# The new stage's norms ahead of the late maxima, POOL's scaled copies spread between the triangles, squares laid out by token

## Time and profile before

| | us |
|---|---|
| median of 3 runs | 1517.89 (1513.53 to 1517.95) |
| profiled execution, its time | 1519.11 |
| its span | 1517.4 |
| PE busy | 1147.0 (76%) |
| DVE busy | 997.9 (66%) |
| ACT busy | 618.4 (41%) |
| POOL busy | 444.8 (29%) |
| mean granted TensorE clock | 0.837 of full speed |

### The profile page before, as it was taken

How to read it: one execution, slowest core, us unless ns; L and a number is a source line. 1 busy time by engine, 2 the same in 40 slices (tenths; PEclk the granted TensorE clock), 3 DMA queues, 4 the chain that set the end, 5 groups by cost and what they waited for, 6 DMA issues and landing times.

```text
span 1517.4 us, 18332 instructions
## 1 busy us (share of the span) xinstructions
PE 1147.0 (76%) x5332; PEld 584.4 (39%) x5332; DVE 997.9 (66%) x2391; ACT 618.4 (41%) x1170; POOL 444.8 (29%) x460
## 2 busy tenths in 40 slices
PE   2778888886886976968878540144988988989897
PEld 1334454452543533525444420122443443434343
DVE  3617336475767668657764756888888888988321
ACT  1070733625626436247165310222463454544552
POOL 2030211203304115124041233234535434434220
PEclk7575888897988988979889775567999989989898
DMA  3111010220320401403103137012021021000000
GB/s 104 58 44 63 30 69 9 96 60 2 128 59 31 125 29 44 139 1 127 51 1 81 30 100 210 21 44 51 7 51 38 21 59 34 24 28 1 21 3 12
DMA packets 85333, 79.81 MB, mean 53 GB/s; under 512 B 42768, under 2 KB 62864, under 8 KB 83216
## 3 DMA queue, kind: packets, MB, share of 16 engines
q1 hardware_dynamic: 85264, 79.01, 18.2%
HBM read 43.45 MB, written 35.00 MB: 52 GB/s over the span
## 4 chain that ended last, share of the span: by engine, by line
PE 58%; DVE 20%; issue 9%; ACT 7%; POOL 3%; SPq 1%; DMA 1%; ACTq 0%; DVEq 0%; POOLq 0%
PE ps L1202 13%; PE ps L1188 9%; PE ps L881 5%; PE ps L943 5%; PE ps L913 4%; DVE arena L1693 4%; ACT arena L1342 3%; PE ps L916 3%; PE ps L972 3%; PE ps L932 3%; PE ps L1194 2%; ACT arena L1304 2%; PE ps L1010 2%; PE ps L992 2%; PE ps L1020 2%
## 5 line engine op out<-in xcount | busy, mean ns | idle before, releaser
L1304 ACT ACTIVATE arena<-ps 128x512 f32<-128x512 f32 (+2 forms) x200 | 110.9, 573 | 336.8 <-PE ps L881 214.3
L1693 DVE TENSOR_REDUCE arena<-ps 128x2 f32<-128x1024 f32 (+3 forms) x176 | 194.6, 1125 | 56.7 <-PE ps L916 54.1
L1202 PE MATMUL ps<-arena,late 128*128 128x512 f32 x512 | 225.6, 592 | 0.0
L1342 ACT ACTIVATE arena<-ps 128x1024 f32<-128x1024 f32 (+3 forms) x256 | 170.2, 718 | 38.9 <-PE ps L932 37.4
L712 POOL TENSOR_SCALAR_AFFINE_SELECT arena<-arena 128x512 f32<-128x512 f32 x128 | 84.8, 667 | 286.0 <-ACT arena L1342 285.7
L881 PE MATMUL ps<-ident,arena 128*128 128x128 f32 (+1 forms) x640 | 114.9, 327 | 48.9 <-ACT arena L1304 15.6
L1188 PE MATMUL ps<-arena,late 128*128 128x512 f32 x256 | 133.6, 682 | 12.4 <-ACT arena L1474 12.4
L1202 PEld LDWEIGHTS ps<-arena,late 128*128 128x128 f32 x512 | 96.2, 190 | 115.8 <-issue 115.5
L913 PE MATMUL ps<-kr,qr 32*128 32x512 f32 (+3 forms) x512 | 107.7, 471 | 35.9 <-issue 20.2
L932 PE MATMUL ps<-qr,kr 32*128 32x256 f32 (+3 forms) x512 | 75.8, 447 | 70.1 <-ACT arena L1342 64.8
L943 PE MATMUL ps<-arena 128*32 128x512 f32 (+3 forms) x1024 | 104.2, 494 | 22.6 <-ACT arena L1304 19.4
(11 more groups left out here) (164 smaller groups left out, 1953.6 us busy)
## 6 DMA issues: line engine op xcount, KB each, us to landing
scan_d<-late SPq DMA_DIRECT2D x64, 138.0 KB, 3.1
qr<-q_rep SPq DMA_DIRECT2D x8, 1024.0 KB, 5.7
kr<-k_rep SPq DMA_DIRECT2D x8, 1024.0 KB, 8.1
arena<-scan_d SPq DMA_DIRECT2D x12, 552.0 KB, 6.0
q_rep<-hilo SPq DMA_DIRECT2D x24, 256.0 KB, 3.0
k_rep<-hilo SPq DMA_DIRECT2D x24, 256.0 KB, 3.9
proj_d<-arena SPq DMA_DIRECT2D x8, 768.0 KB, 5.1
late<-proj_d SPq DMA_DIRECT2D x8, 768.0 KB, 4.4
```

Source lines behind the costliest of these rows:

```text
L1202: last = pe.matmul(ps[:, ring2.bank(f"{n}{c}"), :], w[:, k, c * P:(c + 1) * P], src[:, k, :], start=(k == 0), stop=(k == HC - 1))
L1304: return act.activation(dst, src(ps[:, bank, :]), func, **kw)
L1342: act.activation(prob[:, gg % 2, 2 * pr:2 * pr + 2, p_off[jt]:p_off[jt] + w], ps[:, bank:bank + 2, 0:w], ACT.Exp).then_inc(p_taken, 1)
L1693: v.tensor_reduce(heads[:, 2 * pr:2 * pr + 2, gs[0]:gs[-1] + 1], ps[:, 2 * (k % 2):2 * (k % 2) + 2, 0:len(gs) * w].rearrange("p q (n w) -> ...
```

## The change

On DVE, in slots with both `pre` and `b`, `norms_heads(pre)` moves between the third and the fourth token maximum. In slot 8 (no `b`) the four dispatch copies move ahead of `finish(tail)`, and `norms_heads(pre)` behind it. On POOL, `squares(front)` stands ahead of `scale_keys(pre)`, both at (0, 1); the copies stand one to a place from (0, 1) to (1, 1), and the last score products one place earlier. `p_sq` becomes [2 x 64 tokens][8 features]: POOL reads with a stride and writes in order, and DVE's sum reads in order.

```diff
--- before.py
+++ after.py
@@ -240,7 +240,7 @@
         p_fold_m = p_pairs.rearrange("p c n d -> p (c n d)")
         p_gram = co.take(NC, 6)
         p_fold = co.take(NC, 2 * HD)
-        p_sq = Carve(p_over, late).take(2 * HD, TS)
+        p_sq = Carve(p_over, late).take(2 * TS, HD)
 
 
         c1 = Carve()
@@ -716,7 +716,8 @@
 
                 g.wait_ge(pre_loaded, CREDIT + (b + 1) * 32)
                 g.wait_ge(wy_done, CREDIT + b * DVE_WY)
-                g.tensor_tensor(p_sq, p_mix[:, 0:2 * HD, :], p_mix[:, 0:2 * HD, :], ALU.mult).then_inc(l_squared, 1)
+                qk_p = p_mix[:, 0:2 * HD, :].rearrange("p (w d) t -> p w t d", w=2)
+                g.tensor_tensor(p_sq.rearrange("p (w t) d -> p w t d", w=2), qk_p, qk_p, ALU.mult).then_inc(l_squared, 1)
 
             by_time = lambda j: p_mix[:, j * HD:(j + 1) * HD, :].rearrange("p d t -> p t d")
             along = lambda r: r.unsqueeze(2).broadcast_to([P, TS, HD])
@@ -727,6 +728,8 @@
                 g.wait_ge(norms_done, CREDIT + (b + 1) * DVE_NORMS)
                 g.wait_ge(pre_stored, CREDIT + b * (N2 * 16))
                 g.tensor_tensor(p_kc, by_time(1), along(p_rk), ALU.mult).then_inc(l_kb, 1)
+
+            def fold_keys(b):
                 g.tensor_tensor(p_wu[:, :, 0:HD], by_time(1), along(p_rb), ALU.mult).then_inc(l_kb, 1)
 
             def scale_values(b):
@@ -759,23 +762,27 @@
                     for jt in range(NT):
                         if i is not None:
                             causal(i, gg, jt)
+                        if front is not None:
+                            if (gg, jt) == (0, 1):
+                                squares(front)
                         if pre is not None:
-                            if (gg, jt) == (0, 0):
+                            if (gg, jt) == (0, 1):
                                 scale_keys(pre)
+                            if (gg, jt) == (0, 2):
+                                fold_keys(pre)
                             if (gg, jt) == (0, 3):
                                 scale_values(pre)
+                            if (gg, jt) == (1, 0):
                                 keys_by_depth(pre)
                             if (gg, jt) == (1, 1):
                                 scale_queries(pre)
                             if (gg, jt) == (2, 0):
                                 score_products(pre, (0, 1))
+                            if (gg, jt) == (2, 1):
+                                score_products(pre, (2,))
                             if (gg, jt) == (2, 2):
-                                score_products(pre, (2,))
-                            if (gg, jt) == (2, 3):
                                 score_products(pre, (3,))
                         if front is not None:
-                            if (gg, jt) == (0, 1):
-                                squares(front)
                             if (gg, jt) == QK_TURNED:
                                 low_parts(front)
                 if front is not None:
@@ -1787,7 +1794,7 @@
                 v.wait_ge(l_squared, CREDIT + b + 1)
                 v.wait_ge(l_kb, CREDIT + b * 5)
                 o.mark(v.tensor_scalar(p_beta, p_beta, 0.5, 0.5, ALU.mult, ALU.add))
-                o.step(v.tensor_reduce(p_var, p_sq.rearrange("p (w d) t -> p w t d", w=2), X, ALU.add))
+                o.step(v.tensor_reduce(p_var, p_sq, X, ALU.add))
                 o.step(v.tensor_scalar(p_var, p_var, 1e-6, RSQRT_SCALE, ALU.add, ALU.mult))
                 rsqrt(o, p_r, p_var, p_t)
                 o.mark(v.tensor_tensor(p_rb, p_r[:, TS:2 * TS], p_beta, ALU.mult))
@@ -1834,12 +1841,13 @@
                     steps = fold_heads(pre, o_fold)
                     fold = lambda n: advance(o_fold, steps, n)
                 if moe is not None:
-                    for t in range(NT):
+                    for t in range(3):
                         top(moe, "L", t)
+                    if pre is not None and b is not None:
+                        norms_heads(pre)
+                    top(moe, "L", 3)
                     top(moe, "M", 0)
                     tops = slot_tops(moe)
-                    if pre is not None:
-                        norms_heads(pre)
                 if front is not None:
                     norms(front, (lambda: next(tops, None)) if tops else None)
                 if moe is not None:
@@ -1848,15 +1856,18 @@
                     v.wait_ge(t_act, CREDIT + T.emptied("M3", moe))
                     v.reciprocal(z_inv, z_sum).then_inc(inv_ready, 1)
                     apply_x1(moe)
+                if b is None and moe is not None:
+                    for c in range(4):
+                        take_dispatch(moe, c)
                 if tail is not None:
                     finish(tail)
-                if pre is not None and moe is None:
+                if pre is not None and b is None:
                     norms_heads(pre)
                 if b is not None:
                     attend(b, 0)
-                if moe is not None:
-                    for c in range(4):
-                        take_dispatch(moe, c)
+                    if moe is not None:
+                        for c in range(4):
+                            take_dispatch(moe, c)
                 fold(4)
                 if b is not None:
                     attend(b, 1)
```

## The result

The changed kernel takes 1496.6 us (median of 4 runs, 1491.73 to 1502.47), the kernel before, in the same rounds, 1515.99 (4 runs). The ratio is 0.9875, with a 95% interval of 0.9831 to 0.9918. It is faster, by half of what was predicted (19.4 us for 37.9), and the time lies outside the predicted range of 1469 to 1493. The profiled execution took 1502.47 us (span 1500.8), 16.6 less than that of before (1519.11). The granted clock is 0.835 on average against 0.837.

What follows compares the result with a forecast made beforehand. A once-a-slot ring of waits through POOL, DVE, ACT and TensorE was taken as the bound; 4 x 8.1 + 4.0 + 1.5 = 37.9 us off the profiled 1519.11 gave 1481.2, hence median 1480 us, range 1469 to 1493.

Steps and rivals of the forecast that it cites:

- The ring: Loop slots 3 to 6: waits through POOL, DVE, ACT and TensorE delay the second slot maximum; opening them starts front norms 10.28 us earlier.
- POOL's copies between the triangles: Five scaled copies, one per triangle from (0,1) to (1,1): delay hidden, cost nothing, bounds -0.5 to +1.3 us a slot.
- Rival C: Part of the stall becomes another wait, 2 us a slot more, and the end costs 3: 1493 us, chance 0.18.
- TensorE's clock: Loop slots: without the stall the granted clock falls briefly, taking back 2.2 us, so 8.12 us a slot is saved.
- slot 2's pattern: Clock in the slot without a new stage: three short falls of some 3.4 us each, expected in the loop slots too.
- the difference of 8.12: Predicted saving per loop slot in us: slot 5's period of 102.37 less slot 2's 94.25.
- the whole stall: TensorE's idle stretch before the scores in loop slots; without clock falls, removing it would save 10.3 us a slot.
- rival B: The loop's stall is gained in full, the clock staying high: 10.3 us a slot, 1469 us, chance 0.15.
- Slot 7: No front stage; norms hold up the second slot maximum and TensorE stands 3.74 us; gain 4.0 us, bounds 3 to 5.5.
- Slots 8 and 9: Pipeline's end: gather some 12 us earlier, but the store, load and squares chain limits the gain to 1.5 us, bounds -3 to +3.
- The layout: Squares by token: DVE's reduction 1.22 us for 1.91, POOL's squares 2.0 for 1.90 (bounds 1.9 to 2.8), hidden in slots 3 to 7.
- The sum: Loop, slot 7 and end together: 4 x 8.1 + 4.0 + 1.5 = 37.9 us saved, profiled execution 1481.2, median 1480.

## Why the prediction was wrong

*The ring.* Right in all its steps: the norms in the idle stretch (2.8 us of it left, 2.3 forecast), the squares 0.24 us behind ACT's last copy, the front norms 1.5 us behind the fourth maximum, ACT's wait 10.77 to 0.40 and TensorE's 11.22 to 0.28.

*POOL's copies between the triangles.* This is the step that failed: "All this I cost at nothing (bounds -0.5 to +1.3 a slot)". It was argued from who uses the results, and the results indeed come in time. It left out that POOL's running slows DVE. The front norms alone, from their start to their product, take 4.3 us more than in slot 2 (10.30 - 5.96), and 4.75 us are missing from the period (99.00 - 94.25). Taking the copies' work away brings the product to 6.05, and moving the copies with all their work brings the period to 91.9. So the place of the copies, put at nothing, costs 7.1 us a slot. Only 4.75 of it show against the forecast, because the forecast took off more for the clock than the loop had to pay (below). Rival C had named this ("copies on POOL beside DVE's normalising") with a chance of 0.18 and 2 us a slot; the mechanism was right there and the size less than half, against either figure. The row was at hand: in the earlier trace rows the two copies of keys are over before the front norms begin, since these wait for POOL; opening that wait is what sets them side by side. And slot 5 of before already had one copy beside a normalising step, the queries at 580.93 beside x1's apply (2.84 us); in slot 2, without a copy there, the same four instructions took 1.48:

```profile
270.51 1.48 DVE L1630 TENSOR_SCALAR arena<-arena 128x128 f32<-128x128 f32 x4
...
580.36 2.84 DVE L1630 TENSOR_SCALAR arena<-arena 128x128 f32<-128x128 f32 x4
```

The Trainium skill states the rule (GPSIMD Engine Reference, Specifications): GpSimd's SBUF interfaces are shared with VectorE, with contention where a DVE instruction has two SBUF inputs or runs in a 2-port performance mode. The trace agrees: the two-input steps of the norms go from 0.29 to 1.25 - 1.41 us, while the maxima, which read PSUM, keep 0.68 to 0.69 beside the same copies. No run here shows in which mode an instruction runs; a step with one SBUF input (L1602) stood too. The prediction weighed two other rules of the skill and not this one.

*TensorE's clock.* The forecast took slot 2's pattern over, and read it as three short falls of 3.4 us. Slot 2 of before has a fourth stretch at the low level, about 10 us long (336 to 346): the mean of 0.89 over 94.2 us means 20.7 us at the low level, and three times 3.4 are 10. The loop slots of before have such a long stretch too (643 to 653 in slot 5), so it was in both periods and the difference of 8.12 stands; the account of it by three falls was incomplete.

In the changed kernel the late attention leaves TensorE waiting 4.10 us, the level is 0.50 for all of 579 to 586, and the gather takes 5.21 us. And slot 2's pattern is no constant: the stretch from its front norms to slot 3's took 94.26 us in the changed kernel's profile, 20.7 us of it at the low level by the mean clock (94.26 x 0.11 x 2, since a level of 0.50 takes half off), and 90.87 in that of DVE's order alone, with 10.9 (there the three short falls are absent and the long one is left):

```profile
263.35:357.61 94.26, 82.97 (x525) 44.50 (x524) 56.36 (x128) 47.55 (x90) 18.76 (x22) 0.89 0.20 63
```
```profile
261.36:352.23 90.87, 79.44 (x528) 42.93 (x526) 59.03 (x128) 48.34 (x93) 21.29 (x24) 0.94 0.21 66
```

The place of POOL's copies doesn't decide this. The kernel with the copies moved and the same with slot 8's old order have the same instructions in the same order through slot 7, and slot 2 took 94.27 us in the profile of the one and 89.90 in that of the other; the first reached slot 3's squares at 337.47 and the second at 327.60. What decides it stays open, and two profiles can differ by 10 us at slot 3 without any difference in the instructions before it. The loop slots of these two agree within 1 us each, 91.5 to 92.6, below the 94.25 that were taken as the goal. That is 10.4 us under before's 102.3 on average, as much as the whole stall (10.3). So rival B's gain was there to be had, though not by this order of POOL; part of it comes from copies that stand better than before's did (product at 6.3 for 6.85).

*Slot 7.* 4.0 predicted; from its squares to slot 8's are 82.12 us against 86.02 before, 3.9 less.

*Slots 8 and 9.* A gain of 1.5 predicted; 2.45 measured (109.34 against 111.79 from slot 8's squares to the scan). The mechanism was as put: counted from slot 8's squares, slot 8's norms start 15.1 us later (15.3 predicted), the gather 12.9 us earlier (12 predicted), slot 9's squares come 1.0 us later behind slot 8's (57.34 against 56.35; 1.5 predicted), and DVE's reduction, which stood 5.24 us behind their start, now stands 2.1 behind it. Timelines of POOL and DVE:

```profile
813.79 1.94 POOL L720 TENSOR_TENSOR late<-late 128x1024 f32<-128x1024 f32 x1 [26.60 <-DMA late<-beta_d]
871.13 1.91 POOL L720 TENSOR_TENSOR late<-late 128x1024 f32<-128x1024 f32 x1 [23.27 <-DMA late<-beta_d]
```
```profile
873.24 1.21 DVE L1797 TENSOR_REDUCE late<-late 128x128 f32<-128x1024 f32 x1
```

*The layout.* Reduction 1.21 us (1.22 predicted) for 1.91; squares 1.91 to 1.94 for 1.89 to 1.90, at the low bound; hidden in the loop; at the end it shows as 1.4 us between one profile of each layout.

*The sum.* In the two profiles: slots 3 to 6 gave 13.1 us (396.19 between the squares of slots 3 and 7, against 409.33), where 32.4 were predicted; slot 7 3.9; the end 2.45; up to slot 3 the changed one was 0.4 behind, and the scan and what follows, with the same instructions, took 2.5 more (577.7 against 575.2), which the change doesn't explain; the profiles of the other kernels have 574.3 to 577.5 there. That makes 16.6. Of the missing 21.3 us (1502.5 against 1481.2 for the profiled execution) 19.3 are the loop. They are the failed step, 4 x 7.1 = 28 us by the kernel with the copies moved, less 4 x 2.35 = 9 us by which that loop runs below the forecast's 94.25. The rest is the scan's 2.5 us and the 0.4 before slot 3, less 1 us by which the end beat its forecast.

## What to carry to other kernels

Before moving work of one of the pair POOL and DVE, look at what the other runs at the new place: where DVE has two inputs in SBUF, each side waits for the other's whole instruction in these traces, and "POOL is idle there" is no cover. Put POOL's long instructions beside DVE's idle stretches and its reads of PSUM. When a stall is opened, the stage without it is a forecast only if what the stall kept apart stays apart.

## What the runs showed of the hardware

- DVE instructions with two SBUF inputs and POOL's instructions exclude each other as wholes. L1603 of after, 0.29 us alone, took 1.41 beside a POOL copy of 1.34; L1605 on 128x8, 0.17 alone, 2.21 beside one of 2.36; a POOL product of 32 elements, 0.26 alone, took 1.21 beside a DVE product. POOL's triangles do it as well (L1605 on 128x128 0.67 beside one of 0.64). A single-input DVE instruction on 32-bit data (L1602, 0.21 alone) stood as well, 0.76; the reduction over 1024 elements in SBUF kept 1.21 beside a copy (L1686 at 555.66, POOL's copy from 555.56), and reads of PSUM were untouched.
- POOL's product with both inputs strided by 64 elements took 1.93 us on average, and 1.90 in order (the old layout); DVE's sum over 8 elements took 1.91 us with a step of 64 elements and 1.21 in order.
- The same slot, with the same instructions in the same order, took 94.27 us at a mean granted clock of 0.89 in one profile (copies moved) and 89.90 at 0.94 in another (the same with slot 8's old order).
